# Moving the context's transposes across the value and score products, and the low half to the front of VectorE's step, in a Perceiver layer

## The reference, cut to what matters

```python
# 1. cross attention, 16 heads of 32
q = layernorm(x) @ wq.T + bq
k = ctx @ wk.T + bk
v = ctx @ wv.T + bv
x = x + softmax(q k^T / sqrt(32)) v @ wo.T + bo
# 2. differential self attention, 3. eight gated experts
```

## Time and profile before

| what | value |
|---|---|
| median of 3 runs | 1927.62 us (1927.2 to 1928.88) |
| profiled execution: its time, its span | 1929.77 us, 1927.0 us |
| TensorE matmul busy | 1744.9 us, 91% of the span |
| VectorE, ScalarE, GpSimd busy | 1217.6, 967.0, 730.9 us |
| TensorE's mean granted clock | 0.957 of full speed |

### The profile page before, as it was taken

The page is one execution under the profiler, slowest core; times in us unless marked ns, Lnnn a source line. Parts: engine busy times, 40 slices in busy tenths (PEclk is TensorE's granted clock), DMA queues, the critical chain, the costliest instruction groups (busy, mean ns, idle before and its releaser), DMA issues. The chain is left out here.

```text
span 1927.0 us, 36770 instructions
## 1 busy us (share of the span) xinstructions
PE 1744.9 (91%) x15305; PEld 1374.6 (71%) x15320; DVE 1217.6 (63%) x1407; ACT 967.0 (50%) x1470; POOL 730.9 (38%) x343
## 2 busy tenths in 40 slices
PE   6899999999999999999999999446899689979999
PEld 5677777777777777777777777335788466657886
DVE  5126777777777777777777776885532477853223
ACT  2235665666666666666666666542320387741000
POOL 0002434445445444544543445664000266632220
PEclk9899999999999999999999999657899899989998
DMA  4211110110101101101011100212552432202101
GB/s 158 65 44 27 35 37 29 37 37 28 38 26 37 40 26 37 40 26 37 29 37 37 29 26 4 69 46 91 180 175 82 109 110 89 86 1 66 44 22 44
DMA packets 104188, 104.94 MB, mean 54 GB/s; under 512 B 7263, under 2 KB 72799, under 8 KB 104044
## 3 DMA queue, kind: packets, MB, share of 16 engines
q1 hardware_dynamic: 104044, 102.83, 17.4%
HBM read 79.74 MB, written 23.07 MB: 53 GB/s over the span
## 5 line engine op out<-in xcount | busy, mean ns | idle before, releaser
L515 POOL TENSOR_TENSOR b_acc<-b_acc,b_s 128x1024 f32<-128x1024 f32 x192 | 484.6, 2524 | 297.1 <-ACT b_s L703 284.5
L731 DVE TENSOR_TENSOR b_s<-b_s,b_mb 128x2048 f32<-128x2048 f32 x128 | 356.1, 2783 | 3.5 <-ACT b_mb L690 3.5
L744 DVE TENSOR_TENSOR b_mx<-b_psS,b_mx 128x1024 f32<-128x1024 f32 x224 | 273.9, 1223 | 93.7 <-PE b_psS L585 88.6
L703 ACT ACTIVATE b_s<-b_s 128x2048 f32<-128x2048 f32 x128 | 245.0, 1914 | 165.0 <-DVE b_s L731 164.8
L711 ACT ACTIVATE b_s<-b_psS 128x2048 f32<-128x2048 f32 x128 | 241.4, 1886 | 12.6 <-DVE b_mx L744 12.6
L43 PE MATMUL b_work<-cT,wkT 128*128 128x512 f32 x512 | 214.9, 420 | 22.6 <-ACT b_kT L662 21.1
L510 POOL TENSOR_TENSOR b_acc<-b_s 128x1024 f32<-128x1024 f32 x32 | 76.4, 2388 | 400.9 <-PE b_psO L609 282.1
L43 PE MATMUL b_work<-wvT,cT 128*128 128x512 f32 x512 | 214.6, 419 | 8.8 <-ACT v_sb L683 5.0
L755 DVE TENSOR_TENSOR cT<-b_work,cT 128x512 fp32r<-128x512 f32 x128 | 88.1, 689 | 198.0 <-ACT cT L695 198.0
L44 PE MATMUL b_work<-cT,wkT 128*128 128x512 f32 x512 | 201.6, 394 | 0.0
L45 PE MATMUL b_work<-cT,wkT 128*128 128x512 f32 x512 | 201.0, 393 | 0.0
(11 more groups left out here) (222 smaller groups left out, 3108.7 us busy)
## 6 DMA issues: line engine op xcount, KB each, us to landing
cin<-in_ctx SPq DMA_DIRECT2D x64, 512.0 KB, 3.6
q_scratch<-d_st SPq DMA_DIRECT2D x32, 256.0 KB, 2.5
k_scratch<-d_st SPq DMA_DIRECT2D x32, 256.0 KB, 2.5
e_q<-q_scratch SPq DMA_DIRECT2D x16, 512.0 KB, 3.5
k_sb<-k_scratch SPq DMA_DIRECT2D x64, 128.0 KB, 3.6
experts_sb<-in_L_ffn_expert_w SPq DMA_DIRECT2D x8, 1024.0 KB, 5.2
x_sb<-in_x SPq DMA_DIRECT2D x2, 1024.0 KB, 7.1
q_scratch<-a_q SPq DMA_DIRECT2D x4, 512.0 KB, 3.2
```

Source lines behind the costliest of these rows:

```text
L515: nc.gpsimd.tensor_tensor(acc[:, :, :], acc[:, :, :], s[:, buf, 2 * i:2 * i + 2, :], ALU.add).then_inc(sum_done, 1)
L703: nc.scalar.activation(part, part, ACT.Exp, scale=SCALE).then_inc(exp_done, 1)
L731: nc.vector.tensor_tensor(s[:, n % BUFS, :, :], s[:, n % BUFS, :, :], mb[:, :].rearrange("p (o n) -> p o n", o=1).broadcast_to([P, CHUNK, ...
L744: nc.vector.tensor_tensor(so_far, part, so_far, ALU.max).then_inc(mx_done, 1)
```

## The change

`FIRST` becomes `-SLOT`. `transposed(beat)` counts from it, so every T, its high half on ScalarE and its low half on VectorE stand one beat earlier, in the even beats 0, 2, 4 and 6. On TensorE and ScalarE the code of a beat is unchanged; on VectorE the block of the low half goes from behind the maximum to the head of the beat.

```diff
-        FIRST, LAST = 1 - SLOT, (SLOTS + 4) * SLOT + 3
+        FIRST, LAST = -SLOT, (SLOTS + 4) * SLOT + 3
...
         def _(dve):
             dve.wait_ge(bias_in, 32)
             for beat in range(FIRST, LAST):
+                if (x0 := transposed(beat)) is not None:
+                    p, n = x0
+                    dve.wait_ge(hi_done, p * CHUNK + n + 1)
+                    nc.vector.tensor_tensor(context_place(cT[1], p, n), two(work[RING["T", p, n] % 2]),
+                                            f32(context_place(cT[0], p, n)), ALU.subtract).then_inc(split_done, 1)
                 if (m := spread_slot(beat)) is not None:
...
                     nc.vector.tensor_tensor(fold[:, :, :].rearrange("p j q -> p (j q)"), mx[:, 0, :], mx[:, 1, :],
                                             ALU.max).then_inc(fold_done, 1)
-                if (x0 := transposed(beat)) is not None:
-                    p, n = x0
-                    dve.wait_ge(hi_done, p * CHUNK + n + 1)
-                    nc.vector.tensor_tensor(context_place(cT[1], p, n), two(work[RING["T", p, n] % 2]),
-                                            f32(context_place(cT[0], p, n)), ALU.subtract).then_inc(split_done, 1)
                 if (m := normal_slot(beat)) is not None:
```

## The result

The changed kernel takes 1948.22 us (median of four runs, 1946.43 to 1951.63), the kernel before 1927.41 beside it: ratio 1.0109, 95% interval 1.0091 to 1.0126. It is slower by 20.8 us. The profiled execution took 1948.78 us, its span is 1946.2 us.

The account below looks back on a forecast made before the run. TensorE was taken to set the pace. A slot of 35.05 plus waits of 1.25 and 1.40 makes 37.70 us, 0.97 over 36.73; over 27 slots 26 us, so 1954 us, 1.4% slower, range 1937 to 1968.

Parts of the forecast that it names:

- The four gaps: TensorE's waits at K1, K3, T2 and V3, together 1.58 us a slot, all go.
- V1's wait: V1 on TensorE waits 1.25 us: chain from T2 takes 7.31 us, TensorE's own work 6.06.
- M's wait: M on TensorE waits 1.40 us for the fold, which ends T1 + 9.75, held by GpSimd's adds; own work 8.42.
- The slot without waits: A slot on TensorE without any wait: 36.73 - 1.58 - 0.1 = 35.05 us.
- what the changed neighbours give: Units on TensorE with new neighbours run slightly shorter: four times minus 0.02, minus 0.1 us a slot.
- From slot to total: Slots 4 to 30, 27 of them, each cost 0.97 us more: 26 us in all.
- the first slots have equal gaps in either order: In the first slots, without O and S, TensorE's gaps are the same before and after; no size given.
- The fold did not get ahead of the adds: Rival: fold precedes GpSimd's adds, M doesn't wait, T2 waits 0.8; slot 37.10, 1938 us; chance 0.12.
- The third wait: Rival: subtraction behind T3 held 2.1 us by GpSimd's adds, 0.4 us more each slot; 1965 us; chance 0.10.
- VectorE get ahead of TensorE: Rival: subtraction doesn't hang on the low half; both waits vanish, 1882, or only V1's stays, 1916; chance 0.07.
- The clock: Rival: TensorE, busy 93% of the new slot, loses 2% of granted clock; 19 us more, 1973; chance 0.04.
- GpSimd is held by VectorE too: A slot's first GpSimd add is held by the subtraction behind T0, T0 + 1.93 to T0 + 4.13.

Follow-up runs that it names:

- experiment 1: Changed kernel with every low half on VectorE moved between subtraction and maximum: 1884.93 us, ratio 0.978 to the kernel before.
- experiment 3: Changed kernel with every low half on VectorE moved behind the maximum, ahead of the fold: 1935.71 us, ratio 1.0049 to the kernel before.
- experiment 6: Changed kernel with the low half of T2 alone moved between subtraction and maximum: 1924.75 us, ratio 0.9985 to the kernel before.
- experiment 5: Changed kernel with T1 and T2 back in beats 3 and 5, T0 and T3 still moved: 1889.70 us, ratio 0.9811 to the kernel before.
- experiment 4: Changed kernel with T1 back in beat 3, all other T still moved: 1930.81 us, ratio 1.002 to the kernel before.
- experiment 7: Changed kernel with the low half of T1 alone moved behind the subtraction: 1910.57 us, ratio 0.9907 to the kernel before.
- experiment 8: Changed kernel with six of a slot's seven GpSimd adds cut to 128 of 512 columns: 1889.67 us, one run.
- experiment 2: Changed kernel with every low half on VectorE moved behind the fold, as in the kernel before: 2036.08 us, ratio 1.0562 to that kernel.

## Why the prediction was right

**The four gaps** went, all of them, as forecast.

**V1's wait**: forecast 1.25 from a chain of 7.31 us, measured 1.20 from one of 7.24 (606.92 to 614.16). Experiments 1, 3 and 6 remove it by freeing the subtraction from the low half, experiment 5 by moving T2 back; experiments 4, 7 and 8 leave it alone. The last step, the read-out behind the exp, is read from the rows; no run moved the read-out ahead.

**M's wait**: forecast 1.40, measured 1.81. The mechanism is the one forecast; experiments 1, 3 and 7 remove it by freeing the subtraction from the low half, 4 and 5 by moving T1 back, 8 by shortening the adds, and 6, which changes none of these, keeps it. Of the 0.41 us, 0.25 lie in the chain (10.07 from T1 to M against 9.8: the adds end 0.1 later, M starts 0.15 after the fold and not 0.05), and 0.16 in TensorE's own work, which was shorter than I took it: 8.26 and not 8.42, since K3 stands directly behind K2.

**The slot without waits** was the term mis-sized, in what the changed neighbours give: forecast 0.1, measured some 0.6. I took 2.88 us or more for every projection, as in the rows before, where none stands directly behind another. One that does takes 2.72 (593.67 to 596.39 for K1), and the new order has three such, K1, K3 and V3. That gives 0.48 back: 34.57 instead of 35.05. With 1.81 and 1.20 this is 37.58, against 37.55 measured.

That the slot was forecast within 0.15 us (37.70) is in part luck: this term was 0.48 too high and M's wait 0.41 too low. With the first alone put right the forecast would have been 37.22 us, 13 us over the kernel before instead of 26.

**From slot to total.** Measured 0.82 a slot, 27 slots, 22.1 us; forecast 0.97 and 26. The total moved 20.8. Compared by the reductions behind M, the first is 1.2 us earlier than before (160.79 to 159.58 us), the next slot costs 1.9, the 26 slots up to the last transposes 21.5, and the one that runs out of them gives 1.4 back: 20.8. That the first slots have equal gaps in either order was nearly right, by 1.2 us.

**The rivals.** The fold did not get ahead of the adds: it stood 0.39 us behind them, as worked out. The third wait did not come: the subtraction behind T3 takes 2.28 us. Nor did VectorE get ahead of TensorE: it stands idle for 0.96 and 1.88 us ahead of the low halves of T1 and T2, waiting for ScalarE's high half. The clock stayed at 1.00 in this order, but the rival is real: experiment 2 shows it behind a wait of 2.8 us. The Trainium skill (TensorE: Matmul & The Clock Gate, Part 1) says the clock follows how busy TensorE has been, and that trace agrees with 0.54. The Trainium skill (TensorE: Matmul & The Clock Gate, Engine queue depths) says that ScalarE and VectorE work their queues off strictly in order. The trace agrees: V0's read-out starts at 613.53, behind the exp, though TensorE had gone on to B at 612.43.

## What to carry to other kernels

When a producer is moved up in one engine's order, look at which in-order queues its consumers stand in, and what stands behind them: here the transposes were right to move, and 63 us, from 1948 to 1885, hung on a 0.69 us instruction standing one place too early on VectorE. Put an instruction that waits for fresh work behind one whose inputs are long ready, but not behind one that waits longer itself: between subtraction and maximum the low half gave 1885 us, behind the maximum 1936, behind the fold 2036. A gap may be traded for a chain: follow it to the next unit that waits for its end, with the contention of the instructions on the way: with GpSimd's adds cut short, the same change wins 0.45 us a slot instead of losing 0.82.

## What the hardware showed that was not expected

- That GpSimd is held by VectorE too was forecast from a delay of 0.3 us alone. The change shows it at full size: the first add of a slot (589.95) takes 4.26 us instead of 2.39. It starts 0.30 us after the start of a subtraction with both inputs in SBUF (589.65), which ends at 591.93, and it ends 2.28 us after that.
- After a wait of 2.8 us TensorE's next matmuls ran at a granted clock of 0.54, 4.45 us for a projection of 2.88 (experiment 2). After M's 1.8 us in the changed kernel the clock stayed at 1.00. The fall makes that gap cost 1.6 times itself; where between the two it sets in was not tried.
- A projection directly behind another takes 2.72 us (up to 2.81 where O follows it, K1 of experiments 4 and 5), one behind S, T or B 2.84 to 2.95. Why stays open; no run tried it.
